# Splitting the transposed a of a tile in one copy and one subtraction of 1024 columns instead of two and two of 512

## The reference, cut to what matters

```python
xn = _layernorm(x, axis=-1)
q = (xn @ Wq.T + bq).reshape(b, s, 32, 128)
sig_q = jax.nn.elu(q) + 1.0
q_sel = sig_q[:, :, ::4, :]                       # 8 of the 32 heads are used
num = jnp.einsum('bshd,hde->bshe', q_sel, M)
den = jnp.einsum('bshd,hd->bsh', q_sel, z)[..., None] + 1e-06
retrieved = num / den
out_heads = jnp.repeat(retrieved, 4, axis=2)
attn = out_heads.reshape(b, s, 32 * 128) @ Wo.T
ffn = jnp.einsum('bsd,df->bsf', xn, w.astype(jnp.float32) * w_scale) + b
return x + attn + ffn
```

## Time and profile before

| | |
|---|---|
| median of 3 runs | 237.94 us (237.75 to 238.29) |
| the profiled execution | 237.95 us |
| its span, first to last instruction | 236.1 us |
| outside the span | 1.85 us |
| PE busy | 98% of the span |
| DVE, ACT, POOL busy | 74%, 53%, 45% |
| granted TensorE clock | 1.0 in all slices of the profile |

### The profile page before, as it was taken

The page is one execution under the profiler, slowest core; times in us unless marked ns, Lnnn a source line. Parts: engine busy times, 40 slices in busy tenths (PEclk is TensorE's granted clock), DMA queues, the critical chain, the costliest instruction groups (busy, mean ns, idle before and its releaser), DMA issues.

```text
span 236.1 us, 3421 instructions
## 1 busy us (share of the span) xinstructions
PE 232.5 (98%) x1037; PEld 188.4 (80%) x1037; DVE 174.0 (74%) x275; ACT 125.2 (53%) x285; POOL 107.4 (45%) x117
## 2 busy tenths in 40 slices
PE   8999999999999999999999999999999999999995
PEld 3688788888888788888888888888888888888895
DVE  2989999897589987997858859585667879362511
ACT  4845358687298386585547253654637445630300
POOL 1029437856932356558350442524045598480000
PEclk9999999999999999999999999999999999999999
DMA  6999999999590144471727272431134456879521
GB/s 227 389 412 414 356 250 254 224 212 218 133 278 17 41 95 130 96 180 48 175 89 178 72 196 77 91 104 39 52 94 97 136 135 159 191 189 182 193 98 44
DMA packets 24081, 38.76 MB, mean 164 GB/s; under 512 B 5440, under 2 KB 13248, under 8 KB 22912
## 3 DMA queue, kind: packets, MB, share of 16 engines
q1 hardware_dynamic: 18816, 26.10, 33.7%
q0 software_dynamic: 3808, 11.14, 24.5%
q10 hardware_dynamic: 1440, 1.31, 1.9%
HBM read 25.95 MB, written 4.19 MB: 128 GB/s over the span
## 4 chain that ended last, share of the span: by engine, by line
PE 98%; DVE 0%; issue 0%
PE attn_ps L876 14%; PE attn_ps L878 14%; PE attn_ps L877 13%; PE q_ps L876 10%; PE q_ps L878 10%; PE q_ps L877 10%; PE dense_ps L876 6%; PE dense_ps L878 6%; PE dense_ps L877 6%; PE dense_ps L967 2%; PE q_ps L916 1%; PE q_ps L904 1%; PE q_ps L911 1%; PE attn_ps L916 1%; PE attn_ps L904 1%; PE attn_ps L911 1%
## 5 line engine op out<-in xcount | busy, mean ns | idle before, releaser
L489 ACT ACTIVATE s<-s,rden 128x128 f32<-128x128 f32 x128 | 39.2, 390 | 39.3 <-DVE rden L707 37.6
L341 POOL TENSOR_TENSOR e_and_sz<-s,z_b 128x512 f32<-128x512 f32 x32 | 41.7, 1340 | 39.6 <-DVE den L703 39.6
L876 PE MATMUL attn_ps<-P_hi,aT_hi 128*128 128x512 f32 (+1 forms) x136 | 53.0, 389 | 0.0
L878 PE MATMUL attn_ps<-P_hi,aT_lo 128*128 128x512 f32 (+1 forms) x136 | 52.2, 384 | 0.0
L877 PE MATMUL attn_ps<-P_lo,aT_hi 128*128 128x512 f32 (+1 forms) x136 | 52.1, 383 | 0.0
L876 PE MATMUL q_ps<-WqT_hi,xT_hi 128*128 128x512 f32 x104 | 40.7, 391 | 0.0
L878 PE MATMUL q_ps<-WqT_hi,xT_lo 128*128 128x512 f32 x104 | 40.5, 389 | 0.0
L877 PE MATMUL q_ps<-WqT_lo,xT_hi 128*128 128x512 f32 x104 | 40.5, 389 | 0.0
L691 DVE SCALAR_TENSOR_TENSOR q_ps<-q_ps,rstd,bq_b 128x512 f32<-128x512 f32 x28 | 21.0, 752 | 17.6 <-PE q_ps L878 17.6
L876 PEld LDWEIGHTS attn_ps<-P_hi,aT_hi 128*128 128x128 f32 x136 | 25.6, 188 | 6.1 <-issue 0.6
L878 PEld LDWEIGHTS attn_ps<-P_hi,aT_lo 128*128 128x128 f32 x136 | 25.6, 188 | 5.2
(11 more groups left out here) (96 smaller groups left out, 356.1 us busy)
## 6 DMA issues: line engine op xcount, KB each, us to landing
x<-in_WoT POOLq DMA_DIRECT2D x6, 1024.0 KB, 11.0
x<-in_b POOLq DMA_DIRECT2D x16, 256.0 KB, 4.4
out<-x SPq DMA_DIRECT2D x15, 256.0 KB, 2.4
x<-in_x SPq DMA_DIRECT2D x14, 256.0 KB, 3.6
xT<-in_xT SPq DMA_DIRECT2D x13, 256.0 KB, 3.8
aT<-s SPq DMA_DIRECT2D x104, 32.0 KB, 2.3
MT<-s SPq DMA_DIRECT2D x72, 32.0 KB, 1.9
x<-in_WoT SPq DMA_DIRECT2D x2, 1024.0 KB, 13.3
```

Of the source, the lines that this page charges most:

```text
L341: nc.gpsimd.tensor_tensor(sz_eps[:, :, h * D // 2:(h + 1) * D // 2].rearrange("p g (j c) -> p j g c", j=2), by_quarter(sbuf_s[:, t % SRING ...
L489: last = nc.scalar.activation(a_g, a_g, ACT.Copy, scale=rden[:, t % 2, g:g + 1])
L876: nc.tensor.matmul(out, x_hi, w_hi, start=start, stop=False)
L878: return nc.tensor.matmul(out, x_lo, w_hi, start=False, stop=stop)
```

## The change

The two copies of a tile on ACT become one of 1024 columns, the two subtractions on DVE one of 1024 columns. The semaphores `aT_hi_ready` and `aT_lo_ready` count one per tile where they counted two, so all that wait on them get new numbers; each waits for the same tile as before, except that `split_aT_lo` now starts when the whole copy is done and `product_attn` starts when the whole subtraction is done.

```diff
         def place_free(t):
             if t in (T - 6, T - 5):
                 return xT_lo_ready, t + 5 + (t == T - 5)
-            return aT_lo_ready, 2 * t - (6 if t >= T - 4 else 2)
+            return aT_lo_ready, t - (3 if t >= T - 4 else 1)
...
             def spread_blocks(t):
                 sp.wait_ge(a_turned, t + 1)
                 if t == 1:
-                    sp.wait_ge(aT_lo_ready, 2)
+                    sp.wait_ge(aT_lo_ready, 1)
...
-                for h in range(2):
-                    gs = slice(h * GH, (h + 1) * GH)
-                    nc.scalar.activation(in_groups(aT_hi[:, t % 2, gs, :]), by_head(t, gs), ACT.Copy).then_inc(aT_hi_ready, 1)
+                nc.scalar.activation(in_groups(aT_hi[:, t % 2, :, :]), by_head(t, slice(0, G)), ACT.Copy).then_inc(aT_hi_ready, 1)
...
             def split_aT_lo(t):
-                for h in range(2):
-                    dve.wait_ge(aT_hi_ready, 2 * t + h + 1)
-                    if t >= 2:
-                        dve.wait_ge(attn_filled, t - 1)
-                    gs = slice(h * GH, (h + 1) * GH)
-                    nc.vector.tensor_tensor(in_groups(aT_lo[:, t % 2, gs, :]), by_head(t, gs),
-                                            in_groups(aT_hi[:, t % 2, gs, :]).bitcast(F32), ALU.subtract
-                                            ).then_inc(aT_lo_ready, 1)
+                dve.wait_ge(aT_hi_ready, t + 1)
+                if t >= 2:
+                    dve.wait_ge(attn_filled, t - 1)
+                nc.vector.tensor_tensor(in_groups(aT_lo[:, t % 2, :, :]), by_head(t, slice(0, G)),
+                                        in_groups(aT_hi[:, t % 2, :, :]).bitcast(F32), ALU.subtract
+                                        ).then_inc(aT_lo_ready, 1)
...
                 for g in range(G):
-                    if g % GH == 0:
-                        pe.wait_ge(aT_lo_ready, 2 * t + g // GH + 1)
+                    if g == 0:
+                        pe.wait_ge(aT_lo_ready, t + 1)
...
                 for g in range(G):
-                    if c == 0 and g % GH == 0:
-                        pe.wait_ge(aT_lo_ready, 2 * (T - 1) + g // GH + 1)
+                    if c == 0 and g == 0:
+                        pe.wait_ge(aT_lo_ready, T)
```

## The result

The changed kernel took 238.42 us (median of 20 runs, 238.10 to 239.04) against 237.89 us of before, measured beside it: ratio 1.0022, 95% interval 1.0016 to 1.0029. That is 0.53 us slower. The interval lies above 1, so the loss is there, and the 0.2% at which the prediction drew its line lies inside it. 238.40 us was forecast. The profiled execution took 238.34 us with a span of 236.6 us (236.55 forecast).

A forecast was written before the change was run, and what follows sets the result against it. PE, busy 98% of the span, was taken as the bound, so only stalls between matmuls could move the time. Terms -0.07 + 0.00 + 0.52 = +0.45 us on 237.95 gave 238.40 us, range 237.8 to 238.9.

The forecast's parts named there:

- the 0.2% at which the prediction drew its line: Smallest difference a measurement of this kernel can tell from no change: 0.48 us, 238.42 us; the forecast was just under.
- Tile 9: Merged subtraction held by POOL's second product with z, so PE's load for product_attn(9) is 0.63 us late: 0.52 us lost.
- Tile 8's split: On DVE, would end at 185.78 against 185.79 with add_dense(15) starting as before: zero, but in tile 9's chain.
- Prices: Merged copy 1.046 us, subtraction 1.215 us; a tile saves 0.10 us on ACT and 0.07 us on DVE.
- Tile 0: Shorter split lets PE's load for product_P(6) come earlier, its stall going from 0.23 to 0.16 us: 0.07 us gained.
- The rival of larger savings: Pair as dear as two single instructions, 0.157 us saved a tile; tile 0 gives 0.16, total 238.31 us; chance 0.09.
- Tile 14: Data landing at 219.47, PE can load at 221.89 against 222.38 wanted: 0.49 us left, no loss.
- The rival had a landing 1.0 us later: Tile 14's DMA lands 1.0 us later, PE's load 0.51 late, 0.40 us lost: 238.80 us; chance 0.14.
- Tile 1: Split held to about 96.23, done 0.28 us later at 97.44; product_attn(1) starts at 101.69, cover 4.2 us: nothing lost.
- The sum: Tile 0's -0.07, tile 8's 0.00 and tile 9's 0.52 give +0.45 us on 237.95 us: 238.40 us.

The follow-up runs named there:

- e3: Changed kernel, but copy and split merged at tile 9 alone, all other tiles in halves as before; 238.44 us against 237.91 us of before, ratio 1.0019.
- e7: Changed kernel, but POOL's last product with z (second half of tile 15) done for one group instead of eight; 238.52 us against 238.00 us of before.
- e1: Changed kernel, but only the copy merged, the subtraction in two halves with PE waiting for each; 239.06 us against 237.91 us of before, ratio 1.0055.

## Why the prediction was right, and where it was not

- **Tile 9** carried the forecast, and each number came out: start of the subtraction 193.32 forecast, 193.13 found with all of PE 0.19 us earlier; end 1.09 us behind POOL, 1.08 found; load 0.12 us behind it, 0.11 found; 0.52 us lost, 0.51 found. e3 shows that this tile suffices, e7 that POOL's hold makes the subtraction late. Tile 8's split, put at zero, was so: add_dense behind it starts at 185.51 against 185.70, with PE 0.19 us earlier.
- **Prices**: 1.046 and 1.215 us were forecast for the merged instructions. By tile (duration in ns, min/median/max) the changed kernel has, as in the earlier trace rows,

```profile
L498 ACT ACTIVATE aT_hi<-aT x7: 1044/1046/1062, 71.2 to 211.8; 128x1024 fp32r<-128x1024 f32 x7
...
L720 DVE TENSOR_TENSOR aT_lo<-aT,aT_hi x7: 1211/1226/2024, 74.9 to 212.9; 128x1024 fp32r<-128x1024 f32 x7
```

  The median of the subtraction is 0.01 us above the forecast. The longest, over 2 us, are held by POOL in the loop and cost PE nothing (see the last section).
- **Tile 0** was to give 0.07 us. Timelines of DVE, PE and PEld (compare):

```profile
74.93 1.22 DVE L720 TENSOR_TENSOR aT_lo<-aT,aT_hi 128x1024 fp32r<-128x1024 f32 x1
...
77.59 0.39 PE L874 MATMUL dense_ps<-wd_hi,xT_lo 128*128 128x512 f32 x1
...
77.87 0.19 PEld L872 LDWEIGHTS attn_ps<-P_hi,aT_hi 128*128 128x128 f32 x1 [0.31 <-issue]
```

  The next but one matmul starts at 78.21, 0.62 us after 77.59, where before it was 0.68: 0.06 us gained. The rival of larger savings, 0.16 us here, did not come.
- **Tile 14** was said to keep 0.49 us. It kept none, and PE waited there, which the prediction itself had named as a sign of being wrong. The step that failed is the landing: that of one execution (219.47) was taken as the kernel's. In the changed kernel's profile it was 220.02, and 0.12 us was lost. Between the profiles of the twelve kernels, e1's aside, it goes from 218.5 to 221.0 us, and in four of them it is later than 219.96, where the 0.49 us were used up. The rival had a landing 1.0 us later at 0.14; the two executions at 239.0 us of the changed kernel's twenty fit it, but no profile of them shows it.
- **Tile 1** was called free with 4.2 us of cover. That cover is product_attn(1)'s. The consumer that comes first is another one: the moments of tile 11, which stand behind the held split on DVE and had 0.2 us to spare (finished at 101.23 for a load at 101.44). The changed kernel used it up to no loss, and e1 shows what was 0.2 us away.
- **The sum**: -0.06 + 0.51 + 0.12 = +0.57 us by the profiles, +0.53 measured, +0.45 forecast. In the profiled execution tile 14's 0.12 us and the 0.14 us gained ahead of product_P(6), neither of them forecast, nearly cancel. To that extent it is luck that its 238.34 us lies so near 238.40.

## What to carry to other kernels

Merging two halves of a step is paid by whoever starts on the first half: look at each use for how late the first half already is, and at what stands behind the merged step on its engine, not only at its own consumer. A stall early in a saturated row covers later ones, so take stalls away in the order from the end, or expect half the gain. The landing of a DMA needs several executions before its slack is counted on.

## What the runs showed that was not expected

- DVE and POOL hold each other by whole instructions. With POOL first, DVE's subtraction ends 1.08 to 1.10 us (1024 columns) or 0.54 to 0.56 us (512) behind POOL's end; with DVE first, POOL waits: its centering beside tile 1's subtraction took 2.17 us where 1.29 us is usual.
- The hold of tile 9 is not the only one. In the changed kernel four subtractions of the loop are held in the same way by POOL's centering, 2.02 to 2.03 us each, and PE waits behind none of them, since those splits are made a step ahead. The first of them, and POOL beside it:

```profile
116.31 2.02 DVE L720 TENSOR_TENSOR aT_lo<-aT,aT_hi 128x1024 fp32r<-128x1024 f32 x1
...
115.96 1.29 POOL L316 TENSOR_TENSOR xT<-xT,mean_b 128x512 f32<-128x512 f32 x1 [3.34 <-ACT mean_b L430]
```

- Two short instructions can be riskier than one long one where the other engine waits at the seam: 2.39 us for the pair of tile 1, and again for that of tile 2, in e1's profile, against 1.23 us for the single one in the changed kernel.
- SP's queue issued one DMA behind the other from about 172.8 to 221 us in all these kernels (e1, with PE over 1 us late, from 174.05). The blocks of tile 14 were issued from 208.5 to 210.3 us on, a band of 1.8 us, and landed in one of 2.5 us (218.5 to 221.0); in e1 from 211.6 on, and landed at 221.45. From the first issue to the landing it took 9.2 to 10.8 us in these profiles.
